# An attention and MoE kernel: softmax sums taken from the products' operation instead of matmuls, the norms' last step moved to GpSimd

## The reference, cut to what matters

```python
h = concatenate([tokens_of(x), txt], axis=1)              # (64, 165, 256)
q, k, v = heads(layernorm(h) @ W_qkv.T + b_qkv)
scores = einsum('bhid,bhjd->bhij', q, k) * scale
masked = where(among_the_49_largest, scores, -inf)
attn = softmax(masked, axis=-1)                           # exp / row sum
h = h + einsum('bhij,bhjd->bhid', attn, v) @ W_out.T + b_out
x2 = layernorm(h)
h = h + routed_experts(x2) + (silu(x2 @ Wg) * (x2 @ Wu)) @ Wd
```

## Time and profile before

| | us |
|---|---|
| median of 3 runs | 3195.46 |
| lowest, highest | 3184.11, 3195.62 |
| the profiled execution's own time | 3198.23 |
| its span, first to last instruction | 3196.50 |
| busy: PE, DVE, ACT, POOL | 2648.5, 2591.2, 2482.4, 2208.4 |
| mean granted TensorE clock | 0.923 |

### The profile page before, as it was taken

How to read it: one execution, slowest core, us unless ns; L and a number is a source line. 1 busy time by engine, 2 the same in 40 slices (tenths; PEclk the granted TensorE clock), 3 DMA queues, 4 the chain that set the end, 5 groups by cost and what they waited for, 6 DMA issues and landing times.

```text
span 3196.5 us, 81804 instructions
## 1 busy us (share of the span) xinstructions
PE 2648.5 (83%) x21905; PEld 2103.8 (66%) x21905; DVE 2591.2 (81%) x11585; ACT 2482.4 (78%) x11137; POOL 2208.4 (69%) x4328
## 2 busy tenths in 40 slices
PE   5688888888888888888888888988888888764886
PEld 4466666666677666666666766766666666544875
DVE  1798988888989889898888898888989889842543
ACT  3998898888889888888888888988888889811211
POOL 3567777767777777777777777777777777635665
PEclk7899999999999989999999999999989999877998
DMA  2001000010100010000001010001000000004986
GB/s 64 12 21 24 19 23 19 20 24 18 24 22 18 21 24 20 22 20 23 18 20 24 18 24 23 18 21 24 20 22 20 22 15 20 14 11 133 232 217 134
DMA packets 184208, 119.02 MB, mean 37 GB/s; under 512 B 100304, under 2 KB 175244, under 8 KB 183724
## 3 DMA queue, kind: packets, MB, share of 16 engines
q1 hardware_dynamic: 148864, 93.87, 10.7%
q0 software_dynamic: 34368, 19.34, 3.8%
q10 hardware_dynamic: 492, 0.45, 0.1%
HBM read 66.81 MB, written 33.40 MB: 31 GB/s over the span
## 4 chain that ended last, share of the span: by engine, by line
PE 38%; ACT 25%; DVE 15%; issue 7%; another core or an unknown queue 5%; DMA 4%; POOL 4%; SPq 1%; DVEq 1%; ACTq 0%; POOLq 0%
PE bank L1698 10%; ACT E L852 8%; DVE PR L1253 6%; ACT JK L864 5%; PE bank L1659 3%; DMA out<-E,X 3%; PE bank L1676 3%; ACT JL L877 3%; PE bank L1725 3%; ACT PTT L888 3%; PE bank L1656 2%; PE bank L1627 2%; DVE RD L1258 2%; PE bank L1672 2%
## 5 line engine op out<-in xcount | busy, mean ns | idle before, releaser
L864 ACT ACTIVATE JK<-S,thr 128x165 f32<-128x165 f32 x2688 | 1120.7, 423 | 10.8 <-POOL thr L612 3.4
L671 POOL DMA_INDIRECT slot_token<-TOKI,SLOT x512 | 539.3, 1053 | 224.2 <-issue 192.9
L650 POOL TENSOR_SCALAR X<-S,nt 128x165 f32<-128x165 f32 x1344 | 592.9, 459 | 80.3 <-DVE LIST L1136 71.8
L852 ACT ACTIVATE E<-bank,nb 128x165 f32<-128x165 f32 x1344 | 518.4, 408 | 117.4 <-POOL cnt L632 92.4
L864 ACT ACTIVATION_READ_ACCUMULATOR JK<-S,thr 128x1 f32 x2688 | 513.6, 191 | 0.0
L1253 DVE SCALAR_TENSOR_TENSOR PR<-S,TV,E 128x165 f32<-128x165 f32 x1344 | 455.6, 394 | 0.7 <-PE bank L1676 0.7
L1061 DVE TENSOR_SCALAR_CACHE_REDUCE S<-bank 128x165 f32<-128x165 f32 x1344 | 361.8, 319 | 67.0 <-PE bank L1656 31.9
L1136 DVE MAX8 LIST<-X 128x8 f32<-128x165 f32 x1344 | 351.5, 317 | 7.2 <-DVE X L1126 1.4
L1672 PE MATMUL bank<-IDENT,PR 128*128 128x128 f32 x1344 | 227.3, 287 | 129.4 <-DVEq L1244 71.7
L1126 DVE TENSOR_TENSOR X<-X,flip 128x495 int32<-128x495 int32 x448 | 296.8, 664 | 0.0
L1676 PE MATMUL bank<-IDENT,PR 128*37 128x128 f32 x1408 | 296.6, 293 | 0.0
(11 more groups left out here) (214 smaller groups left out, 6795.8 us busy)
## 6 DMA issues: line engine op xcount, KB each, us to landing
S<-in_w_gate SPq DMA_DIRECT2D x64, 192.0 KB
S<-in_w_up SPq DMA_DIRECT2D x64, 192.0 KB
E<-in_w_down SPq DMA_DIRECT2D x64, 192.0 KB
x_rows<-X SPq DMA_DIRECT2D x64, 160.0 KB
H<-in_txt SPq DMA_DIRECT2D x64, 128.0 KB
QA<-QT SPq DMA_DIRECT2D x512, 10.3 KB
QB<-QT SPq DMA_DIRECT2D x512, 10.3 KB
out<-OT SPq DMA_DIRECT2D x64, 128.0 KB
```

What stands on the lines that cost most here:

```text
L650: last = pool.tensor_scalar(X[n % DEEP][:, t % GROUP, :], S[r % 2][:, t, :], nt[r % 2][:, t:t + 1], DOWN, ALU.add, ALU.mult)
L671: pool.indirect_dma_start(slot_token, bass.IndirectOffsetOnAxis(SLOT[r % 2][:, 0, k:k + 1], 0), TOKI[r % 2][:, :], None, bounds_check=SLOT ...
L852: act.activation(E[r % 2][:, t, :], chunks(bS[g % 3], GROUP, T)[:, t % GROUP, :], ACT.Exp, bias=nb[:, t:t + 1], scale=-1.0, accum_out=sz[: ...
L864: act.activation(JK[:, t % 4, :], S[r % 2][:, t, :], ACT.Sign, bias=(t0, t1)[n][:, t:t + 1], scale=-1.0, accum_out=(c0, c1)[n][:, t:t + 1] ...
```

## The change: what it does

- `mask` and the slow way in `general` get an `accum_out`: each mask product also writes its row sum into a column of den (128 x 21). PE's "sums" products, ONESZ, ONESH and DVE's reciprocal of 128x330 are gone.
- The sums reach the layout of CT in another way, one iteration later: DVE takes the reciprocal of den (`inverse`), PE transposes it (`turned`), ACT copies it to LINE (21 x 128), SP stores LINE to memory (`file_inverses`) and reads it back with each head's row repeated over 16 partitions into RD (`spread_inverses`, two transfers). `back_ctx2` waits for these.
- `diagonal` has a semaphore of its own for each half; half 0 waits for fewer of the scores before. In SP's `iteration` the order is now: file, half 0, spread, half 1, then the stores.
- The last step of both norms is done by POOL, with a negated mean and (add, mult): `front_norm2` behind `front_scale2`, and `back_norm` at the end of the iteration, behind the second `refine2`.
- In `transposes`, ten of the eleven pairs lose the product with the identity: one transpose of 101 columns, which begins 64 columns ahead of the tile's image columns, puts them at rows 64 and up, and the other transpose writes rows 0 to 36 over it afterwards.

```diff
@@ SP @@
             def diagonal(b, half):
                 sp.wait_ge(s_fa, FA * b + 2 + half)
                 gated()
-                ahead(sp, s_score, NG * b, b - 1 if known(b) else b)
+                ahead(sp, s_score, NG * b if half else NG * (b - 1) + MIXED // GROUP + 1, b - 1)
...
+            def file_inverses(b):
+                sp.wait_ge(s_line, b + 1)
+                gated()
+                sp.dma_start(inverses, LINE[:, :]).then_inc(s_filed, 16)
+
+            def spread_inverses(b):
+                sp.wait_ge(s_filed, 16 * (b + 1))
+                gated()
+                ahead(sp, s_bd, BD * (b - 1) + 1, b - 1)
+                gated()
+                rows = inverses.rearrange("t p -> (t p)")[0:ROWS].rearrange("(k h a n) -> h a k n", k=KC, h=HALF, a=1)
+                for k in range(KC):
+                    sp.dma_start(RD[:, k, :], rows[:, :, k, :].broadcast_to([HALF, HD, T])).then_inc(s_rd, 16)
...
+                if has(i - 2):
+                    file_inverses(i - 2)
+                if has(i + 1):
+                    diagonal(i + 1, 0)
+                if has(i - 2):
+                    spread_inverses(i - 2)
+                if has(i + 1):
+                    diagonal(i + 1, 1)
+                if has(i - 3):
+                    store_x(i - 3, (r - 3) % RING)
+                    store_out(i - 3, (r - 3) % RING)
@@ POOL @@
+            def front_norm2(b, r):
+                pool.wait_ge(s_fg, FG * b + 3)
+                ahead(pool, s_fp, FP * (b - 1) + 1, b - 1 if known(b) else b)
+                gated()
+                pool.tensor_scalar(XN[:, 0, :], H[r][:, 0, :], nm[:, 0:1], rs[:, 0:1], ALU.add, ALU.mult).then_inc(s_xn, 1)
+                pool.tensor_scalar(XN[0:IMG, 1, :], H[r][0:IMG, 1, :], nm[0:IMG, 1:2], rs[0:IMG, 1:2],
+                                   ALU.add, ALU.mult).then_inc(s_xn, 1)
...
+                pool.tensor_scalar(bnm[:, :], bmv[:, :, 0], -1.0, None, ALU.mult).then_inc(s_bg, 1)
+
+            def back_norm(b, r):
+                pool.wait_ge(s_bg, BG * b + 3)
+
+                ahead(pool, s_xrow[r % 2], of_ring(b - 2, r % 2, 2, 32), b - 2 if known(b) else b)
+                gated()
+                for c in range(2):
+                    pool.tensor_scalar(X2[r % 2][:, c, 0:D], HM[:, c, :], bnm[:, c:c + 1], brs[:, c:c + 1],
+                                       ALU.add, ALU.mult).then_inc(s_x2, 1)
...
                 if has(i):
                     refine2(i, r, 1)
+                if has(i - 2):
+                    back_norm(i - 2, (r - 2) % RING)
@@ ACT @@
+            def line(b):
+
+                act.wait_ge(s_turned, b + 1)
+                if not known(b) or b:
+                    act.wait_ge(s_filed, 16 * b)
+                act.activation(LINE[:, :], bF[0:NT, 3 * P:4 * P], ACT.Copy).then_inc(s_line, 1)
...
                 if has(i + 1):
                     front_xt(i + 1)
+                if has(i - 2):
+                    line(i - 2)
@@ DVE @@
                 for t in MORDER[lo:hi]:
                     dve.scalar_tensor_tensor(PR[:, t, :], S[r % 2][:, t, :], TV[:, t:t + 1], E[r % 2][:, t, :],
-                                             ALU.is_le, ALU.mult).then_inc(s_prob, 1)
-
-            def back_ctx(b, r):
+                                             ALU.is_le, ALU.mult, accum_out=den[:, t:t + 1]).then_inc(s_prob, 1)
+
+            def inverse(b):
+
+                dve.wait_ge(s_sure, b + 1)
+                dve.wait_ge(s_prob, NT * (b + 1))
+                ahead(dve, s_turned, b, b - 1)
+                gated()
+                dve.reciprocal(inv[:, :], den[:, :]).then_inc(s_inv, 1)
+
+            def back_ctx2(b):
+                dve.wait_ge(s_rd, 16 * KC * (b + 1))
                 dve.wait_ge(s_bp, BP * b + 1)
-                dve.reciprocal(RD[:, :, :], chunks(bY, KC, T)).then_inc(s_bd, 1)
...
                 if has(i):
                     take(i, r, 0)
-                if has(i - 3):
-                    back_norm(i - 3, (r - 3) % RING)
+                if has(i - 2):
+                    inverse(i - 2)
...
-                if has(i + 1):
-                    front_norm2(i + 1, (r + 1) % RING)
@@ PE @@
                 for p in range(2 * n, min(2 * n + 2, PAIRS)):
                     at = P * (p % 4)
-                    pe.transpose(bI[0:IMG, at:at + P], PR[:, p, 0:IMG], IDENT[:, :])
-                    last = pe.matmul(bI[UPPER:UPPER + IMG, at:at + P], PR[:, MIXED + p, 0:IMG], IDENT[:, :],
-                                     start=True, stop=True, skip_group_check=True)
+                    if p == 0:
+                        pe.matmul(bI[UPPER:UPPER + IMG, at:at + P], PR[:, MIXED, 0:IMG], IDENT[:, :],
+                                  start=True, stop=True, skip_group_check=True)
+                    else:
+
+                        hi = (MIXED + p) * T + IMG
+                        pe.transpose(bI[0:UPPER + IMG, at:at + P], rows[:, hi - UPPER - IMG:hi], IDENT[:, :])
+                    last = pe.transpose(bI[0:IMG, at:at + P], PR[:, p, 0:IMG], IDENT[:, :])
...
+            def turned(b):
+
+                pe.wait_ge(s_inv, b + 1)
+                pe.transpose(bF[0:NT, 3 * P:4 * P], inv[:, :], IDENT[:, :]).then_inc(s_turned, 1)
...
                 if has(i + 1):
                     front_xt(i + 1)
                 if has(i - 2):
+                    turned(i - 2)
                     transposes(i - 2, 1)
...
                     transposes(i - 2, 5)
-                    context(i - 2, (r - 2) % RING, "sums")
-                    context(i - 2, (r - 2) % RING, "values")
+                    values(i - 2, (r - 2) % RING)
```

More of the change, by code:

```diff
@@ L104, in early_fusion_kernel @@
         ONES = sb("ONES", [P, P])
-        ONESZ = sb("ONESZ", [P, 2, 2 * HD])
-        ONESH = [sb(f"ONESH{n}", [P, 2, 2 * HD]) for n in range(2)]
         PAD = sb("PAD", [P, 2, NE])
@@ L248, in early_fusion_kernel @@
         s_fp, FP = sem("s_fp"), 4
[L249 removed]
+        s_fd, FD = sem("s_fd"), 3
         s_fa, FA = sem("s_fa"), 6
[L251 to L252 removed]
+        s_fg, FG = sem("s_fg"), 7
+        s_diag, DG = [sem(f"s_diag{n}") for n in range(2)], 16 * HALF
         s_score = sem("s_score")
@@ L1278, in back_aggr @@
                 dve.bn_aggr(bmv[:, 1, :], bst[:, 1, :]).then_inc(s_bd, 1)
-            def back_norm(b, r):
-                dve.wait_ge(s_bg, BG * b + 2)
-                ahead(dve, s_xrow[r % 2], of_ring(b - 2, r % 2, 2, 32), b - 2 if known(b) else b)
-                for c in range(2):
-                    dve.tensor_scalar(X2[r % 2][:, c, 0:D], HM[:, c, :], bmv[:, c, 0:1], brs[:, c:c + 1],
-                                      ALU.subtract, ALU.mult).then_inc(s_bd, 1)
             def back_glu(b):
@@ L1623, in front_qk @@
                     pe.wait_ge(s_wts[1], 16 * 3)
+                if which == 0:
+                    ahead(pe, s_line, b - 2, b - 3 if known(b) else b)
                 for m in range(KC):
```

147 lines of the change are left out of this document (67 added, 80 removed).

## The result

The changed kernel took 3234.88 us (median of 4 runs, 3229.10 to 3238.36) against 3192.73 for the kernel before beside it: a ratio of 1.0135, with an interval of 1.0108 to 1.0162. It is slower by 42 us; the forecast was 3166 and faster, with a range to 3255. The profiled execution took 3229.10 us, 30.9 more than the one of before.

A forecast was written before the change was run, and what follows sets the result against it. The prediction took DVE's chain behind PE's sums as the bound, ACT's ring close behind. Terms -0.6 + 0.3 + 0.2 + 0.1 - 0.5 = -0.5 us an iteration, times 62 = -31, gave 3166 us, range 3095 to 3255.

The forecast's parts named there:

- X2's norm at -0.6: back_norm on POOL behind the second refine2: ACT's gap before X2T shortens, -0.6 us an iteration after 0.1 for POOL's lateness.
- XN's at +0.2: front_norm2 on POOL puts 1.5 us ahead of nine X steps, delaying ACT's third count of group 2: +0.2 us an iteration.
- POOL's true slack: In the slower rival: POOL's wait before bve, 2.1 us a batch, and waits of the same size elsewhere, against 3.1 added.
- The gap ahead of X2T: From ACT's last count to X2T: mean 3.90 us over three turns, forecast to become 3.2 if POOL is in time.
- 0.1 for the clock: PE idles longer ahead of X2's transposes, so its granted clock falls: +0.1 us an iteration, 1 us at the dear end.
- -0.5 for PE: In transposes, PE loses 22 products a batch where ACT waits at VZ: 0.5 us gained, from a range of 0 to 1.2.
- 2.3 at the dearest: DVE's lightening an iteration: 4 us expected, 2.3 if the accumulator reads and small reciprocal cost most.
- the rival in which it goes: ACT's VZ wait vanishes altogether with PE's lighter load: about 3120 us, down to 3085; chance 0.10.
- The rival that came true: POOL's added work or PE's half clock lengthens the ring: up to +1.7 us an iteration, middle 3240 us; chance 0.35.
- point of decision: In the slower rival: POOL reaching the second refine2 0.6 us after ACT's last count.
- three signs: Forecast right if: gap before X2T 3.0 to 3.4 in every iteration, POOL's bmv wait gone, DVE no longer ending last.
- sign of being wrong: Forecast wrong if, among others, PE's granted clock in the batch loop is under 0.9.

The follow-up runs named there:

- norms_dve: Changed kernel with both norms' last steps back on DVE, without nm and bnm: 3023.70 us, 0.9891 of before; on another chip 3076.74 us, 0.9622.
- the load without use: norms_dve with POOL's added norm instructions put back in the same shapes, writing to memory nobody reads: 3201.57 us, 1.0023 of before.
- experiments 16, 17: front_norm2 on POOL moved behind the fourth X group: in the changed kernel 3183.13 us, 1.0399; in it with back_norm on DVE 3086.37, 1.0089.
- 12 to 15: One chip, against before: transposes alone 0.9923; changed kernel with unused PE products 1.0197, with back_norm before second refine2 1.0145; norms_dve with old transposes 0.9951.

## Why the prediction was wrong

**The step that failed** is the price of POOL's added work. The forecast put X2's norm at -0.6 ("The bve wait of POOL vanishes in this") and XN's at +0.2, -0.4 us an iteration together, on the reckoning that it states among the rivals: "POOL's true slack is the bve wait, 135.4 / 64 = 2.1 us, and waits of the same size elsewhere; 3.1 are added". Measured, the two norms cost 5.1% on kind 2 (1.0135 less 0.9622), +2.4 us an iteration by the table, and 5.4% on kind 1 (1.0434 less 0.9891), +2.65, for 2.7 us of instructions.

I priced POOL's work by where it lies on ACT's path. But POOL's own turn closes: nt, X, guess, counts, refine2, nt. Its wait for bmv was not there to be spent, for the rest of the change ends it by itself: norms_dve, with no norm moved, has 37.7 us of it in 5 waits, where the kernel before had 135.4 in 57. The gap ahead of X2T tells the same. The prediction set its 3.2 us against the 3.90 of the kernel before (three turns; the mean over 52, measured in the same way, is 3.6). The rest of the change alone brings that gap from 3.7 to 1.7 us in the table, and the norms on POOL bring it back to 3.4.

**The other parts were mis-sized the other way.** Without the norms the prediction's terms come to -0.1 us (0.3 for LINE, 0.1 for the clock, -0.5 for PE); measured is 43.23 to 41.29, -1.9. So the forecast missed the time by only 2% because one error hid most of the other, and that is luck.

**Durations.** The two groups of the norms, and of what else was added (busy us, mean ns, idle before):

```profile
L675 POOL TENSOR_SCALAR X<-HM,bnm,brs 128x256 f32<-128x256 f32 x128 | 69.7, 548 | 0.5 <-POOL bnm L667 0.5
...
L600 POOL TENSOR_SCALAR XN<-H,nm,rs 128x256 f32<-128x256 f32 x64 | 35.1, 548 | 16.4 <-POOL nm L594 16.4
...
L1297 DVE DVE_READ_ACCUMULATOR PR<-S,TV,E 128x1 f32 x1344 | 106.1, 79 | 0.0
...
L1306 DVE RECIPROCAL inv<-den 128x21 f32<-128x21 f32 x64 | 18.3, 285 | 0.3
...
L939 ACT ACTIVATE LINE<-bank 21x128 f32<-21x128 f32 x64 | 16.1, 252 | 4.8 <-issue 3.9 <-PE bank L1735 0.9
```

The instructions were not mis-sized: POOL's norm steps took 0.55 each where I had 0.62, nm and bnm 0.24 where I had 0.3 (with 0.25 of wait behind nm), the small reciprocal 0.29 (0.2 to 0.3), LINE 0.25 (0.3). X2 on POOL takes 0.548 and on DVE took 47.2 / 128 = 0.37 of busy time, 0.411 in the mean of one. The Trainium skill (GPSIMD Engine Reference, Key points) has Vector about twice as fast for elementwise work, and its section Engine selection says that an operation with one input runs near line rate on GpSimd; these rows, a factor of 1.3 to 1.5, stand nearer to the second. The rule spoke against the move rightly, but not by its factor: the durations were priced about right, and what was missed is whose turn they lengthen.

**DVE.** The 21 accumulator reads show 79 ns each, 1.7 us a batch, but most of that overlaps. Eight mask products with their reads take 2.50 us in the chain of the changed kernel, where eight without took 2.49:

```profile
1379.65 2.50 DVE PR L1297 x16
```

Over the whole trace the mask products with their reads keep DVE busy for 7.6 us a batch, and for 7.1 without them. So 0.5 of the 0 to 1.7 came, 0.8 with the small reciprocal, where 1.0 was taken. By the stretches DVE was busy 38.5 us an iteration and is 36.2, 2.3 less; with the wait of 1.5 for the sums that is near the 4 that were said. ("2.3 at the dearest" doesn't follow from the prediction's own terms, which give 5.0 - 2.0 = 3.0.) DVE did leave the bound: it stands idle ahead of its later takes, and RD's transfers were issued long before CT (at 1368.3, and CT starts at 1379.2 in the iteration shown). SP's part shows no cost.

**PE's gain** was called 0.5 us a batch, "nearer the low end", with the note that the printed releaser does not explain the wait. In the changed kernel on chips of kind 2 ACT's piece from QT to KT lost 0.67, so the size was near. It was not the wait at VZ that gave it, as the prediction had it: that one stayed (77.2 us before, 92.8 after), and with it the rival in which it goes falls. As a part by itself it is larger: 2.6% in norms_dve on one chip of kind 2 (78 us), 0.8% in the kernel before on another. On a chip of kind 1 it was not tried apart from the rest.

**The sums and SP's order**, what is left of norms_dve with the old transposes: 0.9884 and 0.9951 on two chips of kind 2, a gain of 0.5 to 1.2%. That is 0.2 to 0.5 us an iteration (of 43.2), for which the prediction's sum had no term of its own; it counted the reciprocal and the wait for the sums as DVE's, which "leaves the bound".

**The rival that came true** is the slower one, with 0.35 and 3240 us in its middle. Its time was right, and its first half too: POOL. But the time was right in part by luck: it had at most 1.3 us an iteration for the norms where 2.4 came, and hardly a gain of the rest, which was 1.9. Its second half, scores and gate products at half clock, was seen (3.63 us of gate products, TH late), but no run shows that it cost time. Its measure was wrong as well: it asked how late POOL comes to the second refine2 (0.48 us behind ACT's last count in the mean, under its point of decision of 0.6), and POOL had been late all along its turn. Of what was to show the forecast right, three signs came: the gap ahead of X2T was 3.3 in the mean, measured as the prediction does (though not in every iteration: 2.8 to 4.8), POOL's wait for bmv was nearly gone, DVE did not end last. DVE's waits before CT (37.4 us in 35) were not all under 0.5. And one sign of being wrong came too: PE's clock in the loop was 0.89, under 0.9, though norms_dve has it as low. A forecast can be right in its signs and wrong in the time if the signs belong to an engine that only waits.

**Not settled.** What the wait at VZ is that no record of the profile explains, and why it stands in some sessions only. Where the last 1.1% of the norms' cost on kind 2 lie, which the load without use did not bring back. Where the rest of XN's cost lies (experiments 16, 17). And how the changed kernel would do on the chip of 12 to 15.

## What to carry to other kernels

Before work is moved to an engine, go once round that engine's own turn, leg by leg, and ask of each of its waits who ends it; a wait that another part of the same change removes is not slack that can be spent. Read the slack from a kernel that has the rest of the change. Test a ring by load without use at the place in question. Filling a suspect's idle time is a weaker test, since the filling can itself hold up what follows. Here the sums' and the transposes' parts were a gain of 1 to 4%, hidden by a move that cost 5%; parts of a change are worth timing apart.

## What the runs showed of the hardware that was not expected

The kernel before took 3060 us in some sessions and 3166 to 3193 in others, up to 4% more, with less granted clock there (0.947 in the trace of a chip of kind 1, 0.923 in that of kind 2). The traces differ in one thing that stands out: on chips of kind 2 ACT waits at VZ or KT for PE's products in some 20 to 40 iterations, up to 2.9 us at VZ, though PE's records end earlier; on kind 1 it doesn't (77.2 us "remote" against none). Whether that belongs to the chip or to the hour isn't known. The ratio of the same two kernels differed by 3% with it, 1.0135 and 1.0434.

An accumulator read behind a 128x165 mask product on DVE shows 79 ns in the trace and costs far less: eight products with reads took 2.50 us in one place, eight without 2.49, and over the whole trace 21 reads added 0.5 us a batch (7.1 to 7.6) where their own times sum to 1.7.
